# Shorter pauses between GpSimd's pairs of scatters, kept up to block 26

## The reference

```python
x = x + _layernorm(_L0_attn_ref(_layernorm(x), W_qkv, b_qkv, W_out, b_out))
x = x + _layernorm(_L0_ffn_ref(_layernorm(x), Wfc_s, bfc_s, Wproj_s, bproj_s, Wr, Wfc, bfc, Wproj, bproj))
```

```python
logits = xf @ Wr
topk_p, topk_i = jax.lax.top_k(jax.nn.softmax(logits), 2)
topk_p = topk_p / jnp.sum(topk_p, axis=-1, keepdims=True)
for e in range(8):
    h = new_gelu(xf @ Wfc[e] + bfc[e]) @ Wproj[e] + bproj[e]
    routed = routed + h * gate[:, e:e + 1]
return shared + routed
```

## Time and profile before

| | before |
|---|---|
| time, median of 3 runs | 385.84 us |
| lowest and highest | 385.47 and 386.40 us |
| profiled execution: time, span | 386.62, 384.7 us |
| PE busy | 335.6 us, 87% of the span |
| POOL busy | 274.7 us, 71% of the span |
| DVE, ACT busy | 287.0, 256.8 us |
| mean granted TensorE clock | 0.967 of 2.4 GHz |
| pauses (L690) | 21, 436 ns each |
| scatters of lists, of results | 64, 78 |

### The profile page before, as it was taken

One profiled execution on the slowest core, in us unless ns is written; L12 is line 12 of the kernel. 1 busy time (PEld: TensorE's weight loads), 2 busy tenths in 40 slices (PEclk: granted clock), 3 DMA queues, 4 the chain that ended last, 5 costly groups with the idle time before them and its releaser, 6 DMA issues.

```text
span 384.7 us, 8140 instructions
## 1 busy us (share of the span) xinstructions
PE 335.6 (87%) x2497; PEld 291.3 (76%) x2497; DVE 287.0 (75%) x687; ACT 256.8 (67%) x692; POOL 274.7 (71%) x356
## 2 busy tenths in 40 slices
PE   6878787999998998989798888699978999999992
PEld 2537485886976868778598788599967989989961
DVE  4999998999899998999936364565415458777667
ACT  4959865886977967866265674356625666688664
POOL 8778797588788786888767867667664565766640
PEclk9989998999999999999999999699997999999997
DMA  6587567574663425052186359978846779798417
GB/s 192 168 222 211 127 182 114 136 223 93 175 169 101 135 86 155 28 156 72 43 291 212 111 170 222 260 234 259 243 149 190 255 268 382 254 262 259 131 49 206
DMA packets 53521, 69.17 MB, mean 180 GB/s; under 512 B 6365, under 2 KB 37386, under 8 KB 53482
## 3 DMA queue, kind: packets, MB, share of 16 engines
q1 hardware_dynamic: 47556, 58.58, 53.7%
q0 software_dynamic: 4544, 9.35, 7.2%
q10 hardware_dynamic: 1382, 0.79, 0.9%
HBM read 40.06 MB, written 18.15 MB: 151 GB/s over the span
## 4 chain that ended last, share of the span: by engine, by line
PE 35%; DVE 16%; POOL 13%; ACT 12%; issue 9%; another core or an unknown queue 8%; SPq 4%; DMA 3%; POOLq 0%; DVEq 0%; ACTq 0%
PE bO L1549 8%; PE bS L1549 6%; PE bO L1333 5%; DVE KV L1700 3%; POOL expert_lists L706 3%; SPq L423 3%; ACT hs L1152 2%; PE bV L1522 2%; SPq L424 2%; PE bV L1524 2%; ACT hs L1023 2%; PE bV L1523 2%; DMA vr<-vr 2%; DVE Z L1708 1%
## 5 line engine op out<-in xcount | busy, mean ns | idle before, releaser
L829 POOL DMA_INDIRECT expert_results<-yb,yrow x78 | 77.7, 996 | 48.5 <-issue 29.0
L706 POOL DMA_INDIRECT expert_lists<-rows,pos x64 | 64.0, 1000 | 22.8 <-issue 19.9
L1700 DVE TENSOR_TENSOR_SCAN KV<-bS,KV 128x1024 f32<-128x1024 bf16 x32 | 72.8, 2278 | 0.6 <-POOL KV L732 0.3
L1333 PEld LDWEIGHTS bO<-wout_rot,Z 128*128 128x128 f32 x512 | 60.4, 192 | 9.2 <-POOL Z L788 5.2
L1333 PE MATMUL bO<-wout_rot,Z 128*128 128x128 f32 x512 | 62.9, 277 | 3.6 <-POOL Z L788 2.0
L1152 ACT ACTIVATE hs<-bV,KV 128x256 f32<-128x256 f32 x56 | 21.9, 475 | 27.4 <-remote 11.6
L2145 DVE COPY yrow<-xb 128x2 int32<-128x2 int32 x24 | 5.4, 224 | 44.4 <-remote 15.0
L1549 PE MATMUL bO<-KV,hs 128*128 128x128 f32 x232 | 31.0, 281 | 5.9 <-ACT hs L1152 2.8
L1549 PEld LDWEIGHTS bO<-KV,hs 128*128 128x128 f32 x232 | 28.1, 194 | 8.0 <-ACT hs L1152 4.7
L1303 PE MATMUL bA<-w2s_sb,hs 128*128 128x128 f32 x224 | 28.8, 277 | 0.0
L1303 PEld LDWEIGHTS bA<-w2s_sb,hs 128*128 128x128 f32 x224 | 27.1, 192 | 0.2
(11 more groups left out here) (369 smaller groups left out, 989.7 us busy)
## 6 DMA issues: line engine op xcount, KB each, us to landing
KV<-packed_weights SPq DMA_DIRECT2D x21, 578.0 KB
Z<-packed_weights SPq DMA_DIRECT2D x18, 578.0 KB
xb<-expert_lists SPq DMA_DIRECT2D x39, 129.0 KB
vr<-vr SPq DMA_DIRECT2D x16, 224.0 KB, 2.5
shared<-expert_results SPq DMA_DIRECT2D x7, 512.0 KB
vr<-vr SPq DMA_DIRECT2D x16, 192.0 KB
vr<-vr SPq DMA_DIRECT2D x16, 160.0 KB
vr<-vr SPq DMA_DIRECT2D x16, 128.0 KB
```

The lines of the kernel that those rows point to most:

```text
L706: g.indirect_dma_start(out=lists, out_offset=bass.IndirectOffsetOnAxis(ap=pos[:, m:m + 1], axis=0), in_=rows[:, m // TILES, m % TILES, :], ...
L829: g.indirect_dma_start(out=results, out_offset=bass.IndirectOffsetOnAxis(ap=yrow[n][:, c], axis=0), in_=yb[n][:, c, :], in_offset=None).th ...
L1333: ins = t.matmul(bO[:, j * D:(j + 1) * D], Z[:, d, j * P:(j + 1) * P], wout_rot[:, d], start=False, stop=True, skip_group_check=True)
L1700: v.tensor_tensor_scan(w, ps_keep, w, 0.0, ALU.mult, ALU.add).then_inc(s["kv_sum"], 1)
```

## The change

`still` no longer waits after its clearing. It waits ahead of it, for the clearing before, and only then clears. `PAIRED` goes from 12 to 27, so that the pauses follow the pairs of blocks 0 to 26.

```diff
             AT_END = 4
-            PAIRED = 2 * NBUF
+            PAIRED = 27
 
             stills = [0]
 
             def still():
 
+                if stills[0]:
+                    pool.wait_ge(s["stilled"], stills[0])
                 stills[0] += 1
                 g.memset(spare[:], 0.0).then_inc(s["stilled"], 1)
-                pool.wait_ge(s["stilled"], stills[0])
```

## The result

The changed kernel took 389.89 us in the median of 8 runs (387.52 to 391.46), beside 386.40 us for the kernel before (385.47 to 388.26, 8 runs). The ratio is 1.0061, with a 95% interval of 1.0031 to 1.0090: slower by 0.6%, where 384.6 us was forecast. Timed again in two later sessions it gave 1.0066 (1.0032 to 1.0100) and 1.0061 (1.0027 to 1.0094). A run more than 1.5% above the fastest of the same kernel in its session is left out of the ratios: one of e18, and three of the kernel before in the session of e9 to e12, whose median is 387.11 us with them and 386.08 without. The profiled execution took 389.08 us, 2.46 us more than that of before.

What follows compares the result with a forecast made beforehand. PE was taken to bound the kernel, its replies noticed late behind POOL's scatter runs without a long enough rest. The terms +5.3 + 1.6 - 7.2 - 0.9 gave -1.2 us, 384.6 us in the median, range 377.5 to 391.

Steps and rivals of the forecast that it cites:

- 1.: POOL's pauses: rest falls to 0.61 us, period from 3.49 to 2.83 us in blocks 2 to 11; worth nothing by itself.
- 2.: POOL's backlog of blocks 2 to 4 at 241.14: three pairs without a long rest hold PE's replies up, +5.3 us.
- 3.: Ahead of the backlog, before block 1: the last routing's counts reach DVE later as POOL's rest shrinks, +1.6 us.
- 4.: Blocks 16 to 18: the scatter burst at 277 goes as POOL has caught up, and PE's clock holds, -7.2 us.
- 5.: New pauses of blocks 12 to 26: POOL idles anyway, and two late replies at 313.65 and 328.92 may end, -0.9 us.
- The jam at 277: POOL's scatter burst from 277.19 to 286.98, where blocks 16 and 17 took 13.47 us instead of 6.84; forecast to vanish.
- third case: POOL's burst ending at 286.98, followed by PE's late reply at 287.2; cited for replies following scatter ends.
- no wait of over 3 us on ACT or DVE between 255 and 305: Sign in the timelines, behind the backlog: no long wait on ACT or DVE once POOL keeps up.
- the wait near 250: Sign in DVE's timeline: the wait for PE that ended at 242.09 ends near 250 instead.
- A: Lists and blocks: the 0.61 us rest is enough for PE's replies; 376 to 378 us, chance 0.22.
- B: Between blocks 1 and 4: no reply comes through, +8.5 + 2.8 us and a slower clock; 391 us, chance 0.24.
- C: Late replies and scatters only coincide, 385.8 us, chance 0.16; or the wait has a second condition the pauses don't touch.

Runs made afterwards that it cites:

- e18: The changed kernel again, unedited, on another chip with late replies: 391.67 us, ratio 1.0061 to the kernel before.
- e9: The changed kernel again, unedited, in a later session: 388.84 us, ratio 1.0066 to the kernel before.
- e12: The changed kernel with result scatters writing one word of each row instead of 128, results read from x: 422.78 us, one run, chip with late replies.
- e17: The changed kernel with its 0.60 us rest up to block 4 and 1.05 us behind blocks 5 to 26, chip with late replies: 389.55 us, ratio 0.9999.
- e4: The changed kernel with 1200 columns to clear, a rest of 1.27 us in lists and blocks: 393.91 us, ratio 1.0136 to the kernel before.
- e3: The changed kernel with 928 columns to clear instead of 384, a rest of 1.05 us: 388.13 us, ratio 0.9949 to the kernel before.
- e11: The changed kernel with result scatters replaced by clearings of about 1 us, results read from x, chip with late replies: 373.22 us, one run.
- e14: The changed kernel with 0.60 us rest up to block 4, 1.05 us behind blocks 5 to 26, chip without late replies: 373.51 us, ratio 0.9951.
- e10: The changed kernel without any pause in lists or blocks, chip with late replies: 394.68 us, ratio 1.0183 to the kernel before.
- e7: The changed kernel with result scatters replaced by clearings of about 1 us, results read from x, chip without late replies: 371.23 us, one run.

## Why the prediction was wrong

Its steps in order, with what the first profile of the changed kernel has:

1. The shorter pause: right. The clearing is followed by a scatter 0.16 to 0.17 us later, as taken, and the period is 2.83 us.
2. and 3. The backlog of blocks 2 to 4 and the place ahead of it: +5.3 + 1.6 = +6.9 forecast. Measured, block 5's `yb` at 249.8 for 242.2, +7.6 us. The counts reach DVE at 227.59 for 225.90, +1.7. The mechanism and both sizes hold. The sizes rest on a share, 62%, that was read from a single burst, so that they fit to 0.7 us is partly luck.
4. and 5. The gains behind it: -7.2 - 0.9 = -8.1 forecast. Measured, from block 5's `yb` to the end 137.5 for 142.5 us, -5.0.

The sum was -1.2 and is +7.6 - 5.0 = +2.6 us. 0.7 us of the miss of 3.8 us lies in terms 2 and 3, 3.1 us in terms 4 and 5, and there the prediction failed in one claim: "Once POOL keeps up it idles 3.42 - 2.22 = 1.20 us per block", with no late replies to follow. The jam at 277 itself did go: blocks 15 to 21 take 21.6 for 28.4 us, -6.8, though a chain in step would need 20.5. But blocks 5 to 15 take 37.3 for 36.2 us, where nothing was forecast. It is blocks 8 to 15, 25.8 us for 23.9 (7 times 3.42), and that is where the new waits begin. From block 21 to the end it is +0.6 us where term 5 had -0.9: the waits of 313.65 and 328.92 are gone, yet nothing is gained, and why not stays open. A mean of 1.20 us of idle time doesn't mean 1.20 us between every two pairs. After a jam results come in twos, 2.5 to 2.9 us and then 4.1 to 4.7 us apart; their pairs stand 0.60 us apart; that makes the next reply late, and a late reply makes the next two results close. So the pattern seems to feed itself; that is a reading of the rows. What e17 shows is that a longer rest, and nothing else, ends the late replies. In time it was worth 2.1 us in the medians, about two thirds of the 3.1.

The threshold was read wrongly as well. The prediction had replies come through 0.8 to 0.95 us after a scatter's end, but its own third case, 287.22 behind 286.98, is 0.24 us, ACT went on at 281.46 in the middle of that burst, and the three new waits end between 0.16 us before and 0.68 us after one. What length of rest is enough is known only from the runs: 0.72 us wasn't in the lists, 1.05 us was everywhere. In term 3, 62% of 2.8 us is 1.7, not 1.6, which changes nothing.

The new clearings cost DVE as little as was assumed: it is busy for 287.8 us instead of 287.0. That would not have held for longer ones (e4).

In my own list of signs this is the one that failed, "no wait of over 3 us on ACT or DVE between 255 and 305". The others came true: period, clearing to scatter, the wait near 250, and PE over 90% busy from 277 to 292 (93%).

Of the rivals, A (0.60 us is enough) is refuted: e18 and e9 jam where e3 doesn't. B had the right sign and the right place; its price there, 11.3 us, was too high (7.6), and it had no loss behind it. C (the two things coincide) is refuted by e11: without result scatters there is no late reply behind the lists. Its second thought, that there is a further condition, is right in a way that no single trace could show: in two sessions of six there are no late replies at all.

No version was the best everywhere. Where replies are late, 1.05 us in lists and blocks beats both kernels (e3, 0.9949; it wasn't timed elsewhere); where they aren't, 0.60 then 1.05 us does (e14, 0.9951), which is level with before on the other kind (e17, 0.9999).

## What to carry to other kernels

Idle time per period is a mean; ask what the smallest gap is once a hiccup has bunched the work, since a pause that is long enough only on average brings the hiccup back. A longer pause is paid for at the first consumer that waits for the producer's last item (here the read behind block 20: 6 us of lag, 6.4 us of wait), so price both ends before choosing its length. And when a chain holds "remote" waits on a kernel with one core, time it on several chips before tuning against them.

## What was not expected of the hardware

- PE's semaphores were noticed late behind runs of GpSimd scatters, at most after 12.16 us of DVE's wait (e10, until 247.38). Every wait of 2 us or more that "remote" ended stands at an instruction that reads a bank which PE fills. A rest of 1.05 us between pairs ended it, 0.60 and 0.72 us didn't, and 0.87 us stays untried where it matters.
- GpSimd's clearings held DVE's copy of two elements up, in these runs until the clearing's end: 1.88 us behind one of 1.12 us (e4), 5.95 and 8.98 us behind a row of them without a gap (e11, e7), 0.17 us otherwise.
- It depended on the chip, or on the hour: four times present, with the kernel before at 386 to 390 us, twice absent, with 375.9 us both times. No chip came twice among the five sessions of the experiments, so which of the two it is stays open.
- With scatters of one word per row the kernel was 28 us (403.94 for 375.87 us) and 36 us (422.78 for 387.11 us) slower than the kernel before, with fewer bytes to write; one run each.
